# One branch for the whole of TensorE's program, in a macaron block (FFN, attention, FFN)

## The chip, the cores and the metric

The kernel runs on one core of a Trainium2 chip. The metric is the device time of one execution in microseconds (us); three executions of the kernel before gave 636.6, 638.17 and 639.28 us.

## The reference

`x` has 16 sequences of 256 tokens of 128 numbers, all fp32. Biases and weights are inputs; the FFN's weight matrices hold only -1, 0 and 1, each with a scale per output row.

```python
def ffn(x):                                   # _tlin(x, w, s) = einsum('bsi,oi->bso', x, w) * s
    h = silu(_tlin(x, w1_w, w1_s)) * _tlin(x, w2_w, w2_s)      # 128 -> 512
    h = gelu(_tlin(h, h1_w, h1_s), approximate=False)          # 512 -> 512
    h = gelu(_tlin(h, h2_w, h2_s), approximate=False)          # 512 -> 512
    return _tlin(h, w3_w, w3_s)                                # 512 -> 128
x = x + 0.5 * ffn(layernorm(x))
x = x + attention(layernorm(x))               # 16 heads of 8, softmax, projections Wq, Wk, Wv, Wo
x = x + 0.5 * ffn(layernorm(x))
```

## The kernel before

The program is written out by hand, engine by engine: each engine has one block of code, and semaphores join them. All 4096 tokens stay in SBUF (`X`). An FFN works on blocks of 512 tokens, two of them in one `body`; there are four bodies to an FFN, of which the middle two are the two trips of one loop (`Fori`). The attention between the two FFNs goes over 8 pairs of sequences; pairs 2 to 5 are two trips of another loop.

**Split products.** To keep fp32 accuracy each operand of an FFN product is a high part and a low part in a format that TensorE reads in one pass: `act_hi`, `act_lo` for activations, `WH`, `WL` for weights. `split_mm` (line 1014) multiplies `WH` by both parts of the activation. With `general=True` it multiplies `WL` by both as well, which doubles the matmuls. Weights of -1, 0 and 1 have a low part of zero, and then the second half can be left out.

**The flag.** Whether `WL` is all zero is found out while the kernel runs. VectorE takes the largest magnitude of `WL` per partition (`weight_lo_max`, `all_lo_max`), TensorE sums that over the partitions with one small matmul (line 1258), VectorE copies the sum to `flag` (line 730), and TensorE's sequencer loads it into the register `low_weights` (line 1263). The first block's layer 1 is issued ahead of that, always in the general form. Here the flag is zero.

**The branches.** TensorE's FFN code exists twice, as two copies in program order. `ffn_phase` (line 1246) ends in a compare on the register: `If_ne(low_weights, 0)` has the general copy (with `WL`) as its body and comes first in memory, `Else` has the short copy behind it. With a flag of zero the sequencer jumps over the general copy. `ffn_phase` is called once for each FFN, so this occurs twice: once behind the flag (here "branch 1"), once between attention and the second FFN ("branch 2"). Attention's code stands once, between the two. No other engine branches on the flag.

**What orders the work around the branches.** Ahead of branch 1 TensorE has nothing queued but the small sum, since `reg_load` waits for VectorE's copy. Behind it comes `hidden` (line 1048) of the first body: it waits for `h_full`, `h_lo` and `g_hi`, and ScalarE's Gelu (lines 534, 536) frees banks 4 and 5 for its third tile (line 1054). Ahead of branch 2 stand the last 16 `weigh` matmuls of attention (line 1129); behind it comes `layer1` (line 1027) of the second FFN, on `x_hi` and `x_lo` from lines 508 and 776. The sequencer can issue instructions ahead of the matmul array until a wait holds it. At the program's end SyncE stores the last rows of `X` (line 378) and all engines meet at a barrier.

Of the kernel before, what the change touches and what calls it, by code (L numbers as in the profile page):

```python
# [24 lines left out]
I32 = mybir.dt.int32  # L25
# [24 lines left out]
SKEW = 4  # L50
# [11 lines left out]
W_GROUPS = ((0, 1), (1, 2), (2, 3), (3, 5), (5, 7), (7, 9), (9, 11))  # L62
# [3 lines left out]
def macaron_kernel(nc, x, w_ffn, w_att, s12, sg, s3, bqk, bv, bo, eye, sel, low_rows, out):  # L66
# [3 lines left out]
    NBATCH = x.shape[0] // SEQ  # L70
    NPAIR = NBATCH // 2
# [6 lines left out]
    with ctx:  # L78
        def sb(name, shape, dt=F32, c=ctx):
            return c.enter_context(nc.sbuf_tensor(name, shape, dt))  # L80

        def sem(name):
            return ctx.enter_context(nc.semaphore(name))

        bank = [ctx.enter_context(nc.psum_tensor(f"bank{i}", [P, 512], F32)) for i in range(BANKS)]
# [14 lines left out]
        ONES = sb("ONES", [P, 1])  # L100
# [11 lines left out]
        lo_max = sb("lo_max", [P, len(W_GROUPS) + 1])  # L112
        flag = sb("flag", [1, 1])
# [14 lines left out]
        start = ExitStack()  # L128
# [29 lines left out]
        eye_in = sem("eye_in")  # L158
        att_in = sem("att_in")
        w_in = [sem(f"w_in{k}") for k in range(len(W_GROUPS))]  # L160
        ones_set = sem("ones_set")
# [3 lines left out]
        w_lo = sem("w_lo")  # L165
        w_lo_rest = sem("w_lo_rest")
        lo_reduced = sem("lo_reduced")
        flag_sum = sem("flag_sum")
        flag_set = sem("flag_set")
# [85 lines left out]
        def wait(eng, s, v):  # L255

            if not isinstance(v, int) or v > 0:
                eng.wait_ge(s, v)
# [750 lines left out]
        def _(pe):  # L1009
            T = nc.tensor  # L1010
            T.sem_inc(pv_mm, CREDIT)
            MM = T.matmul

            def split_mm(dst, w, xs, general):

                todo = [(wh, part) for (wh, _), (xh, xl) in zip(w, xs) for part in (xh, xl)]
                if general:
                    todo += [(wl, part) for (_, wl), (xh, xl) in zip(w, xs) for part in (xh, xl)]
                for k, (a, b) in enumerate(todo):  # L1020
                    ins = MM(dst, a, b, start=k == 0, stop=k == len(todo) - 1)  # L1021
                return ins

            def w_of(c, t):
                return WH[:, c, P * t:P * t + P], WL[:, c, P * t:P * t + P]

            def layer1(n0, nblk, general, between={}):

                for t in range(L1_TILES):
                    j, n = t // HT, n0 + t  # L1030
                    if t % HT == 0:
                        pe.wait_ge(xlo_done, nblk + j + 1)
                    xs = [(x_hi[:, j, :], x_lo[:, j, :])]

                    last = n - 3 if t >= 3 else n - 2
                    if t != 2:
                        wait(pe, silu_done, last + 1)
                    split_mm(bank[GATE_BANKS[t]][:, :], [w_of(C_W1, t % HT)], xs, general).then_inc(gate_mm, 1)
                    if t != 2:
                        wait(pe, h_full, last + 1)  # L1040
                    split_mm(bank[UP_BANKS[t]][:, :], [w_of(C_W2, t % HT)], xs, general).then_inc(up_mm, 1)
                    if t in between:
                        between[t]()
# [21 lines left out]
            def transpose_x(nx, j, to=None):  # L1065
                pe.wait_ge(xn_done, nx + 1)
                for t in range(TT):
                    ins = T.transpose(bank[to or 6 + j][:, P * t:P * t + P], xn[:, 4 * j + t, :], EYE[:, :])  # L1068
                ins.then_inc(xT_done, 1)
# [173 lines left out]
                    body(i)  # L1243
                body(NP - 1, more=False)

            def ffn_phase(f, low_weights):
                if f == 0:
                    pe.wait_ge(eye_in, 16)
                    transpose_x(0, 0)
                    transpose_x(1, 1)  # L1250

                    pe.wait_ge(w_lo, 2)
                    def sum_low_max():

                        pe.wait_ge(ones_set, 1)
                        pe.wait_ge(lo_reduced, len(W_GROUPS) + 1)
                        MM(bank[6][0:1, 0:1], ONES[:, 0:1], lo_max[:, len(W_GROUPS):len(W_GROUPS) + 1],
                           start=True, stop=True).then_inc(flag_sum, 1)
                    layer1(0, 0, True)  # L1260
                    sum_low_max()
                    pe.wait_ge(flag_set, 1)
                    pe.reg_load(low_weights, flag[0:1, 0:1].bitcast(I32))
                with pe.If_ne(low_weights, 0):
                    ffn_bodies(f, True)
                with pe.Else():
                    ffn_bodies(f, False)

            low_weights = T.alloc_register("low_weights")
            ffn_phase(0, low_weights)  # L1270

            def attend(b, pair, par, bb, prev=True, prev2=True, own=True, more=True, steps=UNITS,
                       ahead=None, v_pair=None):
# [75 lines left out]
            def att_body(i, par, ahead=True, more=True, first=False):  # L1349
                attend(2 * i, i, par, 0, prev=not first, prev2=not first, v_pair=i + 1 if more else None)  # L1350
                attend(2 * i + 1, i, par, 1, prev2=not first, more=more, ahead=i + 2 if ahead else None)

            att_body(0, 0, first=True)
            att_body(1, 1)
            with pe.Fori(1, NPAIR // 2 - 1) as n:
                att_body(2 * n, 0)
                att_body(2 * n + 1, 1)
            att_body(NPAIR - 2, 0, ahead=False)
            att_body(NPAIR - 1, 1, ahead=False, more=False)
            attend(NBATCH, NPAIR, 0, 0, own=False, more=False, steps=SKEW + 4)  # L1360
            ffn_phase(1, low_weights)

# [52 lines left out]
```

## Time and profile before

| | |
|---|---|
| runs of before | 636.6, 638.17, 639.28 us |
| profiled execution, its own time | 636.52 us |
| its span (first to last instruction) | 634.7 us |
| mean granted TensorE clock | 0.986 of full speed |
| PE busy | 597.0 us (94%) |
| ACT busy | 466.7 us (74%) |
| DVE busy | 436.8 us (69%) |
| POOL busy | 94.7 us (15%) |
| chain that ended last | PE 76%, DVE 8%, issue 7% |

PE is TensorE's matmul array and PEld its weight loads, DVE is VectorE, ACT ScalarE, POOL GpSimd, SP SyncE. A q behind a name (PEldq) is that engine's sequencer, whose branches, register loads and drains are recorded but are not counted as busy. "issue" as a releaser means that the engine waited for nothing that the profile shows. In the list of DMA queues, the kind `instruction` is the traffic that loads program code; q8 moved 31 packets of 16 KB.

### The profile page before, as it was taken

Reading aid. Unit: us, or ns where it says so; the run is one execution under the profiler, and the core shown is the slowest. Engines: PE = TensorE matmul, PEld = TensorE weight load, DVE = VectorE, ACT = ScalarE, POOL = GpSimd, SP = SyncE. Lnnn points to the kernel's source line nnn. Section 1 sums busy time; section 2 is a strip of 40 time slices with the busy share of each in tenths; the row PEclk is TensorE's granted clock in tenths of the full one; section 3 lists DMA queues with packets and bytes.
Section 4 is the critical chain, followed back from the end, with each engine's and each line's share of the span. In section 5 each row is a group of like instructions: output and inputs, shape, how many; then the busy total and the mean of one; then the engine's idle time right before and its main releaser. Section 6 shows DMA issues by size and latency. Waiting matters only on the chain.

```text
span 634.7 us, 12980 instructions
## 1 busy us (share of the span) xinstructions
PE 597.0 (94%) x4452; PEld 437.7 (69%) x4452; DVE 436.8 (69%) x1034; ACT 466.7 (74%) x793; POOL 94.7 (15%) x258
## 2 busy tenths in 40 slices
PE   1959999999999999999999999999899999999996
PEld 0738878878776675656656565666578878788785
DVE  4845485667835687979889898896385666855742
ACT  2746796787875568787878878787587877977964
POOL 2702001021010311222222222012001020020000
PEclk9979999999999979999999999999899999999999
DMA  8200000000034073434437062400000001000011
GB/s 287 69 2 2 0 1 1 2 0 0 1 133 133 24 242 124 144 136 133 165 104 263 36 229 106 162 2 2 3 2 0 1 1 35 0 6 27 1 33 35
DMA packets 36674, 41.97 MB, mean 66 GB/s; under 512 B 2448, under 2 KB 27280, under 8 KB 36624
## 3 DMA queue, kind: packets, MB, share of 16 engines
q1 hardware_dynamic: 36624, 41.31, 19.3%
q8 instruction: 31, 0.51, 0.3%
q14 instruction: 19, 0.16, 0.1%
HBM read 22.42 MB, written 18.87 MB: 65 GB/s over the span
## 4 chain that ended last, share of the span: by engine, by line
PE 76%; DVE 8%; issue 7%; POOL 3%; ACT 3%; DMA 2%; POOLq 0%; SPq 0%; DVEq 0%; ACTq 0%
PE bank L1021 48%; PE bank L1129 7%; PE bank L1104 6%; PE bank L1116 3%; PE bank L1118 2%; DVE neg_max L832 2%; PE bank L1161 2%; PE bank L1086 1%; PE bank L1090 1%; DVE act_lo L782 1%; PE bank L1068 1%; PE bank L1147 1%; PE bank L1139 1%; DMA QK<-qk_scratch 1%; DVE silu L791 1%
## 5 line engine op out<-in xcount | busy, mean ns | idle before, releaser
L1021 PE MATMUL bank<-act_hi,WH 128*128 128x512 f32 x576 | 233.1, 405 | 6.6 <-issue 5.3
L1021 PE MATMUL bank<-act_lo,WH 128*128 128x512 f32 x576 | 228.3, 396 | 0.0
L832 DVE TENSOR_REDUCE neg_max<-bank 128x2 f32<-128x512 f32 x256 | 166.2, 680 | 31.8 <-PE bank L1104 30.2
L802 DVE TENSOR_TENSOR act_lo<-full,act_hi 128x512 fp32r<-128x512 f32 x128 | 87.8, 688 | 123.2 <-ACT act_hi L536 123.0
L647 ACT ACTIVATE probs<-bank 128x512 f32<-128x512 f32 x256 | 139.3, 597 | 34.1 <-PE bank L1118 32.3
L534 ACT ACTIVATE full<-bank,SG 128x512 f32<-128x512 f32 x128 | 88.1, 688 | 70.0 <-PE bank L1021 69.6
L1021 PEld LDWEIGHTS bank<-act_hi,WH 128*128 128x128 f32 x576 | 108.7, 189 | 36.8 <-issue 5.9
L1021 PEld LDWEIGHTS bank<-act_lo,WH 128*128 128x128 f32 x576 | 108.8, 189 | 25.1 <-issue 0.5
L1116 PE MATMUL bank<-QK 32*128 32x256 f32 x512 | 93.1, 331 | 0.9 <-DVE m_parts L838 0.5
L536 ACT ACTIVATE act_hi<-bank,SG 128x512 fp32r<-128x512 f32 x128 | 87.4, 683 | 0.0
L1118 PE MATMUL bank<-m_parts,SEL 32*128 32x256 f32 x512 | 79.3, 277 | 0.0
L1104 PE MATMUL bank<-QK 32*128 32x256 f32 x512 | 74.3, 331 | 1.8 <-DVE neg_max L832 1.2
L1104 PEld LDWEIGHTS bank<-QK 32*128 32x128 f32 x512 | 46.1, 185 | 40.4 <-issue 21.1
L1129 PE MATMUL bank<-probs,V 128*32 128x256 f32 x1024 | 69.9, 391 | 0.0
L1116 PEld LDWEIGHTS bank<-QK 32*128 32x128 f32 x512 | 61.4, 185 | 3.6 <-ACT probs L647 2.1
L1118 PEld LDWEIGHTS bank<-m_parts,SEL 32*128 32x128 f32 x512 | 61.9, 187 | 0.0
L791 DVE SCALAR_TENSOR_TENSOR silu<-bank,S,silu 128x512 f32<-128x512 f32 x64 | 47.1, 743 | 16.4 <-ACT silu L521 15.9
L1021 PE MATMUL bank<-x_hi,WH 128*128 128x512 f32 x128 | 51.7, 404 | 2.1 <-issue 1.6
L1021 PE MATMUL bank<-x_lo,WH 128*128 128x512 f32 x128 | 51.1, 399 | 0.0
L521 ACT ACTIVATE silu<-bank,S 128x512 f32<-128x512 f32 x64 | 43.1, 683 | 9.5 <-PE bank L1021 9.5
L399 POOL TENSOR_TENSOR newton<-rstd 128x8 f32<-128x8 f32 (+1 forms) x45 | 11.9, 265 | 241.0 <-DVE rstd L762 238.7
L782 DVE TENSOR_TENSOR act_lo<-silu,act_hi 128x512 fp32r<-128x512 f32 x64 | 45.5, 710 | 0.2
(91 smaller groups left out, 593.2 us busy)
## 6 DMA issues: line engine op xcount, KB each, us to landing
qk_scratch<-qk SPq DMA_DIRECT2D x64, 256.0 KB, 2.6
QK<-qk_scratch SPq DMA_DIRECT2D x16, 1024.0 KB, 7.1
X<-x SPq DMA_DIRECT2D x4, 512.0 KB, 7.2
raw_rest<-w_ffn SPq DMA_DIRECT2D x4, 512.0 KB, 6.0
out<-X SPq DMA_DIRECT2D x4, 512.0 KB, 3.2
raw<-w_ffn SPq DMA_DIRECT2D x3, 256.0 KB, 4.5
WA<-w_att SPq DMA_DIRECT2D x1, 256.0 KB, 5.4
xT<-sel SPq DMA_DIRECT2D x1, 256.0 KB, 5.4
```

The source lines that it names most:

```text
L534: A.activation(full[:, t, :], bank[4 + t % 2][:, :], ACT.Gelu, scale=SG[:, layer, t:t + 1])
L536: A.activation(act_hi[1 + layer][:, j, t, :], bank[4 + t % 2][:, :], ACT.Gelu, scale=SG[:, layer, t:t + 1]).then_inc(g_hi, 1)
L647: A.activation(probs[:, v % 8, :], bank[B_BANKS[bb][v]][:, :], ACT.Exp, scale=SCALE)\
L782: D.tensor_tensor(act_lo[0][:, t // HT, t % HT, :], silu[:, t % SLOTS, :], act_hi[0][:, t // HT, t % HT, :].bitcast(F32), op=ALU.subtract)\
L791: D.scalar_tensor_tensor(out=silu[:, t % SLOTS, :], in0=bank[UP_BANKS[t]][:, :], scalar=S12[:, 1, t % HT:t % HT + 1], in1=silu[:, t % SLOT ...
L802: D.tensor_tensor(act_lo[1 + layer][:, j, t, :], full[:, t, :], act_hi[1 + layer][:, j, t, :].bitcast(F32), op=ALU.subtract)\
L832: D.tensor_reduce(neg_max[:, bb, qt, n0:n0 + 2], bank[(banks or A_BANKS[bb])[u]][:, :].rearrange("p (h k) -> p h k", h=2), axis=AX.X, op=A ...
L1021: ins = MM(dst, a, b, start=k == 0, stop=k == len(todo) - 1)
L1104: ins = MM(bank[banks[u]][:, SEQ * i:SEQ * i + SEQ], q_of(2 * par + bb)[rows, 2 * jj + i, P * qt:P * qt + P], k_of(2 * par + bb)[rows, 2 * ...
L1116: MM(dst, k_of(2 * par + bb)[rows, 2 * jj + i, P * kt:P * kt + P], q_of(2 * par + bb)[rows, 2 * jj + i, :], start=True, stop=False)
L1118: ins = MM(dst, SEL[rows, 2 * jj + i, :], m_parts[rows, bb, :], start=False, stop=True)
L1129: ins = MM(bank[4][32 * h:32 * h + 32, SEQ * (g // 3):SEQ * (g // 3) + SEQ], V[par][:, VROW * (2 * bb + kt) + col:VROW * (2 * bb + kt) + c ...
```

## The change

`ffn_phase` goes. A new function `all_layers(general)` holds the first FFN's bodies, the whole of attention and the second FFN's bodies, and it is written out twice. There is one compare, behind the flag, and its sense is turned: `If_eq(low_weights, 0)` has the short copy as its body, first in memory, and `Else` has the general copy. Nothing else in the kernel is touched; `attend` and `att_body` stay as they are and are only called from another place.

```diff
-            def ffn_phase(f, low_weights):
-                if f == 0:
-                    pe.wait_ge(eye_in, 16)
...
-                    layer1(0, 0, True)
-                    sum_low_max()
-                    pe.wait_ge(flag_set, 1)
-                    pe.reg_load(low_weights, flag[0:1, 0:1].bitcast(I32))
-                with pe.If_ne(low_weights, 0):
-                    ffn_bodies(f, True)
-                with pe.Else():
-                    ffn_bodies(f, False)
...
-            ffn_phase(0, low_weights)
...
-            att_body(0, 0, first=True)
...
-            attend(NBATCH, NPAIR, 0, 0, own=False, more=False, steps=SKEW + 4)
-            ffn_phase(1, low_weights)
+            def all_layers(general):
+                ffn_bodies(0, general)
+                att_body(0, 0, first=True)
+                att_body(1, 1)
+                with pe.Fori(1, NPAIR // 2 - 1) as n:
+                    att_body(2 * n, 0)
+                    att_body(2 * n + 1, 1)
+                att_body(NPAIR - 2, 0, ahead=False)
+                att_body(NPAIR - 1, 1, ahead=False, more=False)
+                attend(NBATCH, NPAIR, 0, 0, own=False, more=False, steps=SKEW + 4)
+                ffn_bodies(1, general)
...
+            layer1(0, 0, True)
+            sum_low_max()
+            pe.wait_ge(flag_set, 1)
+            pe.reg_load(low_weights, flag[0:1, 0:1].bitcast(I32))
+            with pe.If_eq(low_weights, 0):
+                all_layers(False)
+            with pe.Else():
+                all_layers(True)
```

**Branch 1, on TensorE, before.** `bank4` takes the first tile of the first hidden layer; the rows between are the same pair for the other three blocks of the sum.

```order
L1258 MATMUL bank6<-lo_max,ONES 1x1
L1263 TENSOR_LOAD flag
L1264 COMPARE_AND_BRANCH
L1021 MATMUL bank4<-act0_hi,WH 128x512
L1021 MATMUL bank4<-act0_lo,WH 128x512
...
L1021 MATMUL bank4<-act0_hi,WL 128x512
L1021 MATMUL bank4<-act0_lo,WL 128x512
```

**Branch 1, on TensorE, of the change.**

```order
L1251 MATMUL bank6<-lo_max,ONES 1x1
L1356 TENSOR_LOAD flag
L1357 COMPARE_AND_BRANCH
L1021 MATMUL bank4<-act0_hi,WH 128x512
L1021 MATMUL bank4<-act0_lo,WH 128x512
...
L1021 MATMUL bank5<-act0_hi,WH 128x512
L1021 MATMUL bank5<-act0_lo,WH 128x512
```

Before, the general copy (with `WL`) follows the compare, and the copy that runs here stands 1,062 rows of the list further on. In the change the copy that runs here follows the compare at once.

**Branch 2, on TensorE, before.** The end of attention and layer 1 of the second FFN; `probs,V1` are the `weigh` matmuls of the last sequence but one step.

```order
L1154 MATMUL bank6<-EYE,o_nat 128x128 x2
L1161 MATMUL bank6<-WA,onT 128x128 x2
L1129 MATMUL bank4<-probs,V1 32x256 x8
L1264 COMPARE_AND_BRANCH
L1021 MATMUL bank0<-x_hi,WH 128x512
L1021 MATMUL bank0<-x_lo,WH 128x512
L1021 MATMUL bank0<-x_hi,WL 128x512
```

**The same place in the change.**

```order
L1154 MATMUL bank6<-EYE,o_nat 128x128 x2
L1161 MATMUL bank6<-WA,onT 128x128 x2
L1129 MATMUL bank4<-probs,V1 32x256 x8
L1021 MATMUL bank0<-x_hi,WH 128x512
L1021 MATMUL bank0<-x_lo,WH 128x512
L1021 MATMUL bank2<-x_hi,WH 128x512
```

The compare has gone, and the short form of layer 1 follows attention directly.

**The end of the copy that runs here, in the change.** The last transposes of the output, and what follows them in memory.

```order
L1074 MATMUL bank6<-EYE,yT 128x128 x4
L1074 MATMUL bank7<-EYE,yT 128x128 x4
L1357 UNCONDITIONAL_BRANCH
L1021 MATMUL bank4<-act0_hi,WH 128x512
```

The short copy now ends in a branch over the whole general copy (3,349 rows of the list) to the program's end. Before, the short copy of the second FFN was the last thing in TensorE's program.

## Rows read from the trace of the kernel before

**Rows 1.** The page's first part: busy time, share of the span, instructions.
```profile
PE 597.0 (94%) x4452; PEld 437.7 (69%) x4452; DVE 436.8 (69%) x1034; ACT 466.7 (74%) x793; POOL 94.7 (15%) x258
```

**Rows 2.** What PE waited for: releaser, us in total, times, longest us.
```profile
PE bank L1068 <- DVE xn L770: 13.4, 1, 13.4
PE bank L1021 <- issue: 6.9, 2, 5.3
PE bank L1139 <- POOL neg_max L450: 2.8, 6, 0.8
```

**Rows 3.** Timeline at branch 1: start, us, engine, line [idle before <-releaser].
```profile
33.18 0.74 DVE L791 SCALAR_TENSOR_TENSOR silu<-bank,S,silu 128x512 f32<-128x512 f32 x1
34.73 0.19 PE L1258 MATMUL bank<-lo_max,ONES 128*1 128x1 f32 x2 [1.72 <-DVE lo_max L725]
35.77 0.14 DVE L730 COPY flag<-bank 1x1 f32<-1x1 f32 x1
40.25 0.76 PE L1021 MATMUL bank<-act_hi,WH 128*128 128x512 f32 x1 [5.32 <-issue]
...
43.80 0.49 PE L1021 MATMUL bank<-act_hi,WH 128*128 128x512 f32 x1
44.07 1.28 ACT L534 ACT_TABLE_LOAD   x1 [8.16 <-PE bank L1021]
45.36 0.69 ACT L534 ACTIVATE full<-bank,SG 128x512 f32<-128x512 f32 x1
45.95 0.68 ACT L536 ACTIVATE act_hi<-bank,SG 128x512 fp32r<-128x512 f32 x1
46.68 0.51 PE L1021 MATMUL bank<-act_hi,WH 128*128 128x512 f32 x1 [0.76 <-ACT act_hi L536]
```

**Rows 4.** Both compares on the flag, and the flag's load: ns min/median/max, first and last start.
```profile
L1264 PEldq COMPARE_BRANCH  x2: 3300/3440/3579, 36.5 to 451.3; - x2
L1263 PEldq TENSOR_LOAD <-flag x1: 492/492/492, 35.9 to 35.9; - x1
```

**Rows 5.** The loops' compares on PE's sequencer, FFN and attention, same columns.
```profile
L1242 PEldq COMPARE_BRANCH  x4: 76/156/243, 125.8 to 591.1; - x4
L1355 PEldq COMPARE_BRANCH  x2: 83/159/235, 335.4 to 392.8; - x2
```

**Rows 6.** DMA queues in 36 to 42 us: queue, kind, packets, MB.
```profile
q8 instruction: 2, 0.03, 2.2%
```

**Rows 7.** DMA queues in 334 to 395 us, all that moved anything.
```profile
q1 hardware_dynamic: 7031, 9.44, 44.2%
```

**Rows 8.** Timeline at branch 2.
```profile
449.34 0.69 DVE L776 TENSOR_TENSOR x_lo<-bank,x_hi 128x512 fp32r<-128x512 f32 x1 [0.29 <-ACT x_hi L508]
450.09 1.28 ACT L521 ACT_TABLE_LOAD   x1
451.27 1.94 PE L1129 MATMUL bank<-probs,V 128*32 128x256 f32 x16
454.76 0.47 PE L1021 MATMUL bank<-x_hi,WH 128*128 128x512 f32 x1 [1.56 <-issue]
455.50 0.69 ACT L521 ACTIVATE silu<-bank,S 128x512 f32<-128x512 f32 x1 [4.13 <-PE bank L1021]
```

**Rows 9.** PE's busy time and clock by stretch: us, busy (x), PEclk, DMA share, GB/s.
```profile
37.20:40.20 3.00, 0.00 (x0) 0.50 0.02 5
40.25:43.90 3.65, 3.65 (x9) 0.50 0.02 4
44.00:46.00 2.00, 1.92 (x8) 1.00 0.00 0
450.20:453.50 3.30, 3.01 (x20) 0.50 0.02 7
60.00:120.00 60.00, 59.98 (x271) 1.00 0.00 1
```

**Rows 10.** The end: timeline, the last store's landing, and the drains at the barrier.
```profile
629.52 0.66 PE L1074 MATMUL bank<-EYE,yT 128*128 128x128 f32 x4 [0.34 <-ACT yT L543]
631.11 0.38 SPq L378 DMA_DIRECT2D out<-X  x1
L78 PEldq DRAIN  x1: 700/700/700, 629.5 to 629.5; - x1
L78 SPq DRAIN  x1: 7/7/7, 634.5 to 634.5; - x1
```

More of the change, by code:

```diff
@@ L1244, in ffn_bodies, with sum_low_max @@
                 body(NP - 1, more=False)
-            def ffn_phase(f, low_weights):
-                if f == 0:
-                    pe.wait_ge(eye_in, 16)
[L1249 to L1259, printed above, removed]
-                    layer1(0, 0, True)
-                    sum_low_max()
-                    pe.wait_ge(flag_set, 1)
-                    pe.reg_load(low_weights, flag[0:1, 0:1].bitcast(I32))
-                with pe.If_ne(low_weights, 0):
-                    ffn_bodies(f, True)
-                with pe.Else():
-                    ffn_bodies(f, False)
-            low_weights = T.alloc_register("low_weights")
-            ffn_phase(0, low_weights)
+            def sum_low_max():
+                pe.wait_ge(ones_set, 1)
+                pe.wait_ge(lo_reduced, len(W_GROUPS) + 1)
+                MM(bank[6][0:1, 0:1], ONES[:, 0:1], lo_max[:, len(W_GROUPS):len(W_GROUPS) + 1],
+                   start=True, stop=True).then_inc(flag_sum, 1)
             def attend(b, pair, par, bb, prev=True, prev2=True, own=True, more=True, steps=UNITS,
@@ L1351, in att_body @@
                 attend(2 * i + 1, i, par, 1, prev2=not first, more=more, ahead=i + 2 if ahead else None)
-            att_body(0, 0, first=True)
[L1354 to L1359, printed above, removed]
-            attend(NBATCH, NPAIR, 0, 0, own=False, more=False, steps=SKEW + 4)
-            ffn_phase(1, low_weights)
+            def all_layers(general):
[9 more added lines that the diff above has]
+                ffn_bodies(1, general)
+            low_weights = T.alloc_register("low_weights")
+            pe.wait_ge(eye_in, 16)
+            transpose_x(0, 0)
+            transpose_x(1, 1)
+            pe.wait_ge(w_lo, 2)
+            layer1(0, 0, True)
[6 more added lines that the diff above has]
+                all_layers(True)
 def kernel(**inputs):
```

## The prediction, made before the changed kernel was run

> **What bounds the kernel now.** I read the busy shares first. PE is busy 597.0 of 634.7 us, 94% of the span, with 4,452 matmuls [rows 1]. TensorE is the bound, and 37.7 us of idleness are all there is to win without touching its matmuls. Then I read what PE waited for [rows 2]. The largest entry, 13.4 us, is the start (loads and the first layer norm), which the change doesn't touch. The next is "issue", 6.9 us in only two pieces, 5.32 and 1.56 us. "issue" means that no semaphore explains it, so the reason has to be sought in the instruction stream. The timeline puts one at 40.25 us, right behind the flag [rows 3], the other at 454.76 us, between attention and the second FFN [rows 8]. These are the places of the two compares on the flag. The sequencer's own records then give the cause its size: the two compares take 3579 ns (at 36.5 us) and 3300 ns (at 451.3 us) [rows 4]. The reader should set beside them the loops' compares on the same engine. In each group one execution goes back to the loop's head and the next leaves the loop: maxima of 243 and 235 ns, minima of 76 and 83 ns [rows 5]. So a compare that falls through costs about 80 ns, a short jump back about 240 ns, and only the long jump over the general copy costs 3.3 to 3.6 us.
>
> What is in these 3.3 to 3.6 us? In 36 to 42 us the queue that loads program code moves two packets of 16 KB [rows 6]. The whole second trip of the attention loop, 334 to 395 us, has no such packet at all [rows 7], although its body is hundreds of matmuls long. I read that as: code that lies behind the sequencer is still there, code that lies far ahead has to be fetched when the jump is taken, and the sequencer stands still meanwhile.
>
> **Branch 1, step by step.** The flag's copy starts at 35.77 us, the register load at 35.9 takes 492 ns, the compare starts at 36.50 and ends 3.58 us later, at 40.08 [rows 3, 4]. The first matmul behind it starts at 40.25, 0.17 us on. In the change the copy that runs follows the compare. It takes 0.08 us as the loops' exits do, so the first matmul starts at 36.50 + 0.08 + 0.17 = 36.75 us: 3.50 us earlier. Nothing else is late at that time. `hidden` needs the sixth product of layer 1, done at 33.18 + 0.74 = 33.92 us [rows 3]; its low parts for the first block are older.
>
> What follows is a chain from PE's first tile: 8 matmuls, then ScalarE's table load (1.28 us, which starts only when the tile is there), two Gelu passes, and PE's third tile at 46.68 us, which waits 0.76 us for them [rows 3]. From the first matmul to that is 46.68 - 40.25 = 6.43 us. It moves as a whole if the tile takes as long as before. Its 8 matmuls ran at half clock: the granted clock was 0.50 from 37.2 to 43.9 us after PE had stood idle, and 1.00 from 44.0 [rows 9]. At 0.50 they took 43.80 - 40.25 = 3.55 us; at full clock, by the 60 us stretch with 271 matmuls in 59.98 us (0.221 us each) [rows 9], they take 1.8 us. With a shorter pause the clock may fall as before, or not fall. Two ends: the second tile also runs slow and its 8 matmuls last past the Gelu, some 3.55 + 3.55 - 6.43 = 0.7 us lost; or the first tile runs fast, 3.55 - 1.8 = 1.75 us won. I take 0: PE is idle here for nearly 4 us in the change too, and the row that I have shows a fall. Branch 1 gives 3.5 us, between 2.8 and 5.2.
>
> **Branch 2.** The compare starts at 451.29 and ends at 454.59, but PE still has 16 queued matmuls until 451.27 + 1.94 = 453.21 us [rows 4, 8]. That covers 1.9 us of the jump, and 1.56 us are left bare. Without a compare layer 1 starts at 453.2. Its input `x_lo` was ready at 449.34 + 0.69 = 450.03, and ScalarE's table load, which would be next late, ended at 451.37 [rows 8]. ScalarE and VectorE wait 4.13 us here for PE [rows 8], so they move with it. The clock stood at 0.50 until 453.5 [rows 9], so a first matmul may run slow at a cost of 0.2 us. Branch 2 gives 1.5 us, between 1.2 and 1.6.
>
> **Does the gain last?** Between the two PE is saturated (59.98 of 60 us in mid-FFN [rows 9]), and every other engine is released by PE's results. The loads of the start were done before 36 us. An earlier PE thus moves everything behind it by the same amount.
>
> **The end.** The short copy now ends in a long jump. PE's sequencer is through at 629.5 us and drains in 0.70 us [rows 10]. A jump of 3.3 to 3.6 us brings it to 633.1 at most, its drain no later than 633.8. The barrier waits for the last store anyway: issued at 631.11, SyncE's drain at 634.5 [rows 10]. 0.7 us of cover are left, all of it shifted alike by the gains above. I cost the jump at 0; bare, it would cost at most what it takes beyond 4.3 us. Attention's second copy is never executed and costs nothing but memory.
>
> **Sum.** 3.5 + 1.5 = 5.0 us from this execution's span of 634.7 gives 629.7, and from its own time of 636.52 gives 631.5. This execution lies 1.65 us below the median of the runs, 638.17. From the median the same gain gives 633.2 us, 0.8% faster.
>
> **A figure that speaks against it.** The Trainium skill ("Advanced Engine Details and Errata", Control Flow Timing) gives a compare-and-branch about 108 ns. By that figure two compares are worth 0.2 us, and the change nothing. The loops' rows of 76 to 243 ns are near it, the two rows of 3300 and 3579 ns are not, so the trace disagrees where the jump is long. The skill's "Runtime: NRT & Kernel Launch", Instruction fetch mechanics, says that a taken branch forces a fetch when its target is outside a window of two pages. The trace agrees on the fetch but not on so small a window: an attention trip of 57 us came back to its head in 235 ns without a packet.
>
> **Rivals.**
> 1. *The compare's time is not the jump* but the price of a compare right after work that was waited for, and stays where it is at branch 1. For: branch 1 stands behind a register load. Against: branch 2 has no load ahead of it and costs 3.30 us all the same [rows 4]. Or the code right behind branch 1 is not loaded yet; against that, no code packet is asked for until 37 us, and none of the many later steps from one packet's code to the next shows as "issue" [rows 2]. Either way only branch 2 is won: 638.2 - 1.5 = 636.7 us, "no change". Chance 0.08.
> 2. *A cheap compare.* The two pauses are something else that stays, and the time is 638.2 us. It is the result that the 108 ns of the page would give. The pairing of rows 4 with both "issue" gaps speaks against it. Chance 0.03.
> 3. *Loops that lose their code* (the slower side). The loops now lie elsewhere. If their heads had been dropped when they branch back, each of the three back edges (125.8, 335.4, 548.0 us) would cost 3.3 to 3.6 us instead of 0.24, of which PE's queue covers up to 1.9 us: 1.4 to 3.3 us bare, 4.2 to 9.9 us in three. Against a gain of 5.0 this gives -0.8 to +4.9 us, in the middle 640 us. It makes the kernel slower by over 3.2 us when more than 2.7 us a back edge are bare. It is what the skill's window of two pages would do to any body longer than that. For it: nothing in the trace. Against: the bodies keep their length, and the longest came back in 235 ns [rows 5, 7]. Chance 0.03.
> 4. *The end comes bare*: the last jump's fetch runs beside the last store and takes 2 us longer than its cover. The gain is then 3.0 us, 635.2 us. Chance 0.06.
>
> **How the numbers follow.** My forecast, both gaps gone, has 0.80. About 0.5% (3.2 us) is what a measurement of this kernel can tell from no change. The forecast's own range of gains is 4.0 to 6.8 us by the bounds above; nearly all of it lies beyond 3.2 us, but the three runs of before spread by 2.7 us, so I keep 0.03 of it for "same". Faster: 0.77 + 0.03, half of rival 4, = 0.80. Same: 0.03 + 0.08 (rival 1) + 0.03 (rival 2) + 0.03 (the other half of rival 4) = 0.17. Slower: 0.03 (rival 3). The range runs from 638.2 - 6.8 - 0.4 for the runs' spread = 631.0 to 636.8, which takes in rivals 1 and 4.
>
> **What would show it right or wrong.** In the changed kernel's records the one compare on the flag should last about 0.1 us; the gap behind the small sum should be about 1.8 us in place of 5.32, the gap behind the last `weigh` matmuls gone, and "issue" no longer among PE's largest waits. An unconditional branch of 3 to 4 us should stand at the end, with PE's drain before SyncE's. The loops' maxima should stay near 240 ns. A compare that is still over 3 us long, loop compares of over 1 us, or PE's drain as the last at the barrier would each refute a step. The forecast fails as a whole if the span is above 632 us.

## The result, and the profile after

| | runs | median us | ratio to before, 95% interval |
|---|---|---|---|
| before | 5 | 638.17 | |
| the change | 5 | 630.43 | 0.9881 [0.9852, 0.9909] |
| before, measured again | 19 | 637.16 | |
| the change, measured again | 6 | 630.32 | 0.9908 [0.9885, 0.9931] |

The change makes the kernel 0.9 to 1.2% faster in the two measurements, 6.8 to 7.7 us between medians. I had forecast 633.2 us, 5.0 us faster, with a low end of 631.0: the direction was right, the size too small, and the time lies below my range. The first profiled execution of the change took 645.56 us, and the ratio leaves it out; what happened in it is told below. The rows here are from the profiled execution of the second measurement, with a span of 627.9 us against 634.7.

What PE waited for there (us in total, times, longest us), to be read against [rows 2]:

```profile
PE bank L1068 <- DVE xn L770: 13.3, 1, 13.3
PE bank L1139 <- POOL neg_max L450: 2.9, 6, 0.8
PE bank L1251 <- DVE lo_max L725: 1.9, 1, 1.9
PE bank L1021 <- DVE silu L791: 1.8, 1, 1.8
```

"issue" has left the list. In its place at branch 1 stands a gap of 1.8 us, put down to a VectorE product. In truth it is the way of the sum through the flag's copy on VectorE, the register load and the compare. The sequencer's compares, to be read against [rows 4, 5], and the drains at the end against [rows 10]:

```profile
L1357 PEldq COMPARE_BRANCH  x2: 93/1892/3692, 36.5 to 622.7; - x2
L1242 PEldq COMPARE_BRANCH  x4: 76/153/233, 122.1 to 584.3; - x4
L1339 PEldq COMPARE_BRANCH  x2: 83/152/220, 331.4 to 388.8; - x2
L78 PEldq DRAIN  x1: 67/67/67, 626.5 to 626.5; - x1
L78 SPq DRAIN  x1: 7/7/7, 627.7 to 627.7; - x1
```

The compare on the flag takes 93 ns at 36.5 us. The record of 3692 ns at 622.7 us is the branch over the general copy at the end. It is through before PE's drain at 626.5, 1.2 us ahead of SyncE's, so it is hidden.

The two places, on PE's timeline and ScalarE's (start, us, engine, line [idle before <-releaser]), against [rows 3, 8]:

```profile
34.69 0.19 PE L1251 MATMUL bank<-lo_max,ONES 128*1 128x1 f32 x2 [1.95 <-DVE lo_max L725]
36.72 0.76 PE L1021 MATMUL bank<-act_hi,WH 128*128 128x512 f32 x1 [1.84 <-DVE silu L791]
...
40.33 1.28 ACT L534 ACT_TABLE_LOAD   x1 [4.46 <-PE bank L1021]
...
42.94 0.50 PE L1021 MATMUL bank<-act_hi,WH 128*128 128x512 f32 x1 [0.82 <-ACT act_hi L536]
...
446.93 1.07 PE L1129 MATMUL bank<-probs,V 128*32 128x256 f32 x16
447.93 0.50 PE L1021 MATMUL bank<-x_hi,WH 128*128 128x512 f32 x1
```

The first hidden tile starts at 36.72 us (forecast 36.75) in place of 40.25, and the third at 42.94 in place of 46.68: 3.74 us won. At branch 2 layer 1 starts 1.00 us behind the start of the last `weigh` matmuls, in place of 454.76 - 451.27 = 3.49 us. The `weigh` group itself takes 1.07 us, not 1.94: its clock was whole here.

The two traces also tell where the gain comes in. The change leads by 3.74 us at the third tile, by 451.27 - 446.93 = 4.34 us at the last `weigh` group, and by 454.76 - 447.93 = 6.83 us at layer 1 of the second FFN. The spans differ by the same 6.8 us, so the whole gain is there once branch 2 has been passed, and 2.49 us of it come at branch 2 itself. The 0.6 us between the two branches fall partly where before ran at half clock already (450.2 to 453.5 us [rows 9]) and the change did not.

### The profile page after: what moved, and what is told of

Same layout as the page of the kernel before. It is cut to its first block, busy times and chain, and to the rows that moved or that the text cites. A ratio compares the mean times of both kernels' runs of the same rounds, so it can differ in the third digit from the quotient of the medians.

```text
span 643.8 us, 12980 instructions
## 1 busy us (share of the span) xinstructions
PE 604.8 (94%) x4452; PEld 443.5 (69%) x4452; DVE 437.8 (68%) x1034; ACT 466.4 (72%) x793; POOL 94.7 (15%) x258
## 4 chain that ended last, share of the span: by engine, by line
PE 73%; DVE 7%; issue 7%; DMA 4%; POOL 3%; ACT 3%; SPq 1%; POOLq 0%; DVEq 0%; ACTq 0%
PE bank L1021 47%; PE bank L1129 6%; PE bank L1104 6%; PE bank L1116 3%; PE bank L1118 2%; DMA QK<-qk_scratch 2%; DVE neg_max L832 2%; PE bank L1161 1%; PE bank L1086 1%; PE bank L1068 1%; SPq L340 1%; PE bank L1090 1%; DVE silu L791 1%; DVE act_lo L782 1%; PE bank L1139 1%
## 5 line engine op out<-in xcount | busy, mean ns | idle before, releaser
L1116 PE MATMUL bank<-QK 32*128 32x256 f32 x512 | 97.0, 341 | 0.9 <-DVE m_parts L838 0.5
L1104 PE MATMUL bank<-QK 32*128 32x256 f32 x512 | 77.1, 341 | 8.9 <-issue 6.7
L1118 PE MATMUL bank<-m_parts,SEL 32*128 32x256 f32 x512 | 82.4, 285 | 0.0
L1104 PEld LDWEIGHTS bank<-QK 32*128 32x128 f32 x512 | 48.4, 193 | 48.9 <-issue 27.8
L1116 PEld LDWEIGHTS bank<-QK 32*128 32x128 f32 x512 | 64.2, 193 | 3.7 <-ACT probs L647 2.1
L1118 PEld LDWEIGHTS bank<-m_parts,SEL 32*128 32x128 f32 x512 | 64.9, 196 | 0.0
```

The costliest lines, as they stand in the source:

```text
L1104: ins = MM(bank[banks[u]][:, SEQ * i:SEQ * i + SEQ], q_of(2 * par + bb)[rows, 2 * jj + i, P * qt:P * qt + P], k_of(2 * par + bb)[rows, 2 * ...
L1116: MM(dst, k_of(2 * par + bb)[rows, 2 * jj + i, P * kt:P * kt + P], q_of(2 * par + bb)[rows, 2 * jj + i, :], start=True, stop=False)
L1118: ins = MM(dst, SEL[rows, 2 * jj + i, :], m_parts[rows, bb, :], start=False, stop=True)
```

## The experiments

Each kernel is given by its edit; all medians are device times of one execution.

**The change once more.** No edit.

> The changed kernel once more, for its usual time and a second trace. In its first profiled execution (span 643.8 us) the compare at the end of the attention loop's first trip took 5113 ns instead of 235 ns, with code packets all through the second trip, and TensorE's clock then stood at half for 20 us. Theory L (layout): the loop now lies so that its code and the block fetched ahead of it don't fit at once, in every execution; then this trace shows the compare at 3 to 5 us again, and the median of 630.4 us contains that loss. Theory C (chance): it was an accident of that one execution; then this trace shows about 235 ns, no code packet in the second trip, and a span of 627 to 630 us. Theory K (clock): what the change gained beyond 5.0 us is less time at half clock after shorter pauses; then the mean granted clock is above 0.986 here, and span differences follow it.

Median 630.32 us (629.69 to 633.64), before 637.16 beside it. The attention loop's compare took 220 ns (row above), so "in every execution" of theory L is refuted. Theory K holds in part: this trace has a mean clock of 0.991 against 0.986. Grouping the executions by their mean clock gives a rough split. At 0.989, before has spans of 634.4 us (mean of 16) and the change, padded or not, 628.55 us (mean of 4): 5.9 us are gone at equal mean clock. The other 1 us goes with a higher mean clock, 0.9889 against 0.9853 over 16 and 42 executions. But the mean counts idle time too. Before stood at half clock for some 3 us in which PE did nothing (37.2 to 40.2 us [rows 9]); by an estimate, half of 3 us over a span of 634.7 us, that alone lowers its mean by 0.0024 and costs nothing. So how much of the last 1 us is the clock's is not shown.

**One branch, general copy first.**

```diff
-            with pe.If_eq(low_weights, 0):
-                all_layers(False)
-            with pe.Else():
-                all_layers(True)
+            with pe.If_ne(low_weights, 0):
+                all_layers(True)
+            with pe.Else():
+                all_layers(False)
```

> One branch only, but with the general copy first and the old sense (If_ne): branch 1 keeps its long jump, branch 2 is gone, the end needs no jump. By the prediction's steps 1.5 us under before, 636.7 us, with a compare of 3.3 to 3.6 us at 36.5 us. If branch 1 is worth more than its 3.5 us through the clock, this kernel stands 5 us or more above the changed one; if the extra gain comes from having one branch at all, it is within 3 us of the changed one.

634.50 us (633.23 to 636.06), ratio 0.9953 [0.9937, 0.997]. Branch 2 alone is worth 637.16 - 634.50 = 2.7 us, not 1.5; branch 1 is the remaining 4.2 us, between the two cases that I had set (5 us or more, and within 3 us). The 2.7 us can't be put down to the mean clock: this kernel idles at branch 1 as before does, and at a mean clock of 0.989 its two executions have spans of 631.6 us, 2.8 us under before's 634.4. The compare at branch 1 is as long as ever:

```profile
L1357 PEldq COMPARE_BRANCH  x1: 3686/3686/3686, 36.4 to 36.4; - x1
```

PE's timeline at the place where branch 2 was:

```profile
451.10 1.16 PE L1161 MATMUL bank<-WA,onT 128*128 128x128 f32 x4 [0.62 <-ACT onT L661]
452.19 1.94 PE L1129 MATMUL bank<-probs,V 128*32 128x256 f32 x16
454.05 0.74 PE L1021 MATMUL bank<-x_hi,WH 128*128 128x512 f32 x1
```

In this execution the clock was at half here although there is no jump, so the fall of the clock at attention's end is not the jump's doing. It comes in some executions and not in others. With it layer 1 starts 1.86 us behind the `weigh` group's start, without it 1.00 us.

**Before, moved by 70 instructions.**

```diff
                     pe.wait_ge(eye_in, 16)
+                    for _ in range(140):
+                        pe.wait_ge(eye_in, 16)
```

 Theory L: its compare at the loop's end rises from 235 ns to 3 to 5 us, code packets appear in the second trip, and the time rises by 2 to 5 us to 640 to 643 us, more where the clock falls. Theory C: no difference, 638 us, and 235 ns.

639.29 us (636.53 to 649.27), ratio 1.0028 [1.0006, 1.005]: slower than before by little, between the values of the two theories. The loop's compare took 231 ns in the profiled execution (640.00 us), so the miss did not come there. Three of the 12 executions took 642.21, 642.85 and 649.27 us; they have no trace, so whether the miss came in them is open. By the count of instructions the loop's end lies 4 short of where I wanted it, at the edge and not beyond it; the kernel tests theory L badly. Its trace is worth more at branch 2. PE's timeline, and then its clock by stretch (us, busy, PEclk):

```profile
453.19 1.07 PE L1129 MATMUL bank<-probs,V 128*32 128x256 f32 x16
456.92 0.77 PE L1021 MATMUL bank<-x_hi,WH 128*128 128x512 f32 x1 [2.66 <-issue]
```

```profile
456.80:459.90 3.10, 2.98 (x7) 0.50 0.03 5
460.30:462.00 1.70, 1.70 (x11) 1.00 0.00 0
```

Here the `weigh` group runs at full clock and is over after 1.07 us. So the jump's bare part is 2.66 us in place of 1.56 [rows 2, 8], and the clock is at half behind it, when layer 1 starts. From the group's start to layer 1 it is 3.73 us (before: 3.49). This is what branch 2 costs: the sequencer's 3.3 to 3.5 us set that interval in both traces, with the `weigh` group at half clock in one and at full clock in the other.

**The change, moved by 40 instructions.**

```diff
             pe.wait_ge(eye_in, 16)
+            for _ in range(80):
+                pe.wait_ge(eye_in, 16)
             transpose_x(0, 0)
```

> The changed kernel with 80 waits on a semaphore that is already up, at TensorE's start, where it is idle until 13.3 us: they cost nothing and move all later code by 40 instructions, so that the attention loop crosses one fetch boundary fewer (6 as before, not 7). Theory L: the compare at the attention loop's end falls from 3 to 5 us to about 0.24 us, the second trip has no code packets, and the time falls by 2 to 5 us under the changed kernel, to 626 to 628 us. Theory C: no difference, 630 us within noise.

630.56 us (628.39 to 631.41): no difference from the change, as it has to be if the change's usual executions don't miss either. Loop compare 222 ns.

**The change, moved by 16 instructions.** The same edit with 32 waits.

> The changed kernel moved by only 16 instructions (32 waits at TensorE's idle start). In the changed kernel a fetch boundary falls within a few instructions of the attention loop's closing compare, by counting instructions and by when the code packets came; here it falls some 16 ahead of it in every execution, while the loop's head stays in the same block as in the changed kernel. Theory L (the loop's code plus the block fetched ahead exceed what TensorE keeps): each execution now misses at the back edge: a compare of 3 to 5 us in the first trip's end, 7 more code packets in the second trip, and a median of 633 to 645 us. Theory C (the miss in the change's first profiled execution was unrelated to layout): 235 ns, 630.5 us.

641.28 us (639.21 to 648.6) in 12 executions, ratio 1.0067 [1.0036, 1.0098]: slower than before, and some 11 us above the change. Even the fastest is 5.6 us above the slowest of the change's ten other executions (633.64). The profiled execution, the only one with a trace: first the loop's compare, then what PE waited for and the first matmul behind the jump, then the code packets from 334 to 402 us and from 337.9 to 341.7 us, then the clock by stretch:

```profile
L1339 PEldq COMPARE_BRANCH  x2: 83/2371/4659, 333.2 to 402.6; - x2
```

```profile
PE bank L1104 <- issue: 7.6, 1, 7.6
341.74 0.57 PE L1104 MATMUL bank<-QK 32*128 32x256 f32 x1 [7.64 <-issue]
```

```profile
q8 instruction: 8, 0.13, 0.8%
q8 instruction: 1, 0.02, 1.5%
```

```profile
336.40:353.00 16.60, 11.26 (x92) 0.50 0.55 182
354.00:370.00 16.00, 15.93 (x206) 1.00 0.01 2
```

The jump back to the loop's head takes 4659 ns, eight packets of code come in the second trip where before had none [rows 7], and PE stands bare for 7.6 us. The jump explains only the first half of that: it ends at 333.16 + 4.66 = 337.8 us, and the next matmul comes 3.9 us later. One more packet of code comes in that second half. That the block behind the head's was missing as well is my reading of it; no run shows it apart. The clock stays at half for some 17 us, to 353 us at least. In the first profiled execution of the change the jump back takes longer still, and PE stands bare twice, for 4.48 and 2.17 us:

```profile
L1339 PEldq COMPARE_BRANCH  x2: 83/2598/5113, 333.2 to 404.2; - x2
338.62 0.57 PE L1104 MATMUL bank<-QK 32*128 32x256 f32 x1 [4.48 <-issue]
342.14 0.37 PE L1104 MATMUL bank<-QK 32*128 32x256 f32 x1 [2.17 <-issue]
336.50:356.80 20.30, 16.01 (x116) 0.50 0.48 156
```

So theory L holds with one correction: in the change a fetch boundary falls on the loop's last instructions, and by their times (645.56 us against 628.70 to 633.64) the miss came in 1 of its 11 executions; 16 instructions further on the median is 11 us higher; 40 further on, by the count, the head has moved into the next block too, and the usual time is back. No experiment shows what decides it at the edge from one execution to the next.

**Before with only branch 2 turned.**

```diff
+                if f == 0:
+                    with pe.If_ne(low_weights, 0):
+                        ffn_bodies(f, True)
+                    with pe.Else():
+                        ffn_bodies(f, False)
+                else:
+                    with pe.If_eq(low_weights, 0):
+                        ffn_bodies(f, False)
+                    with pe.Else():
+                        ffn_bodies(f, True)
```

> The kernel before with only branch 2 turned to If_eq, so that it is still there but falls through. Theory J (only the long jump costs): branch 2 lasts about 0.08 us and the kernel equals the one with one branch and the general copy first, which measured 634.5 us. Theory N (a compare of any kind stops TensorE's queue): it stays at before's 637.2 us.

634.80 us (633.69 to 638.2), before 638.03 on the same chip at the same time, ratio 0.9961 [0.9939, 0.9982]: 3.2 us, as with no branch 2 at all (0.9953). A compare that falls through costs PE nothing here. It takes 79 ns at 451.8 us, and layer 1 starts 1.00 us behind the `weigh` group's start, as in the change. The 3474 ns are its jump at the end, hidden.

```profile
L1270 PEldq COMPARE_BRANCH  x2: 79/1776/3474, 451.8 to 627.6; - x2
451.79 1.07 PE L1129 MATMUL bank<-probs,V 128*32 128x256 f32 x16
452.79 0.50 PE L1021 MATMUL bank<-x_hi,WH 128*128 128x512 f32 x1
```

**Both branches kept, both turned.** `If_eq` with the short copy first in `ffn_phase`, for both FFNs.

> Both branches kept and both turned to If_eq. Both compares fall through; in exchange the first FFN's short copy ends in a long jump to attention, behind the transposes of its last output. Theory J: the two compares take under 0.1 us, the new jump 3.3 to 3.8 us on the sequencer, of which TensorE's queue covers little there; so one jump price comes back and the time is 633 to 635 us, 3 to 4 us above the changed kernel. If the sense of the branch alone carried the gain, it would be 630.5 us.

630.89 us (628.75 to 632.0), ratio 0.9884 [0.9851, 0.9916]: the change's own time. My forecast of a jump price at the end of the first FFN was wrong. The jump is there (four records at this line, the longest 3839 ns), but on PE's timeline it leaves no "issue":

```profile
L1264 PEldq COMPARE_BRANCH  x4: 75/1864/3839, 36.6 to 625.0; - x4
215.15 1.09 PE L1074 MATMUL bank<-EYE,yT 128*128 128x128 f32 x8
217.44 0.51 PE L1104 MATMUL bank<-QK 32*128 32x256 f32 x4 [1.19 <-DVE neg_max L832]
218.02 0.41 PE L1139 MATMUL bank<-EYE,neg_max 128*128 128x128 f32 x2
```

The same place in the change:

```profile
216.73 0.51 PE L1104 MATMUL bank<-QK 32*128 32x256 f32 x4 [0.44 <-DVE neg_max L832]
218.06 0.41 PE L1139 MATMUL bank<-EYE,neg_max 128*128 128x128 f32 x2 [0.83 <-POOL neg_max L450]
```

The jump starts at 213.25 us, while PE has work until 215.15 + 1.09 = 216.24; 1.2 us are left bare. The change waits there for other engines anyway, 0.44 and 0.83 us, and the matmul behind starts at 218.06 us with no jump and at 218.02 with it. One branch in place of two is therefore not what gained: which copy stands first is.

**A version that beats both.** The first seven matmuls of the first hidden tile are the same in both copies. They go ahead of the small sum and the flag, and the copies begin with the eighth (on top of the move by 40).

```diff
+            def hoisted():
+                pe.wait_ge(silu_done, 6)
+                pe.wait_ge(h_lo, HT)
+                pe.wait_ge(g_hi, 1)
+                w = [w_of(C_H1 + k, 0) for k in range(HT)]
+                todo = [(wh, part) for (wh, _), (xh, xl) in zip(w, inputs_of(0, 0)) for part in (xh, xl)]
+                for k, (a, b) in enumerate(todo[:HOISTED]):
+                    MM(bank[4][:, :], a, b, start=k == 0, stop=False)
...
             layer1(0, 0, True)
+            hoisted()
             sum_low_max()
```

> A version meant to beat both: the changed kernel, moved by 40 instructions as in the padded version, with the first 7 matmuls of the first hidden tile (they are the same in both copies) issued ahead of the small sum and the flag, into the 1.7 us in which TensorE waits for the largest low part. The tile is then complete 0.2 us behind the branch instead of 3.6, so ScalarE's table load and Gelu start earlier. By the second trace of the changed kernel: its first tile ends at 40.3, here at about 37.2, so third tile and all behind it come 2.5 to 3.1 us earlier, and 627.5 to 628.5 us. If a clock that falls later takes the gain back (TensorE still idles 1.8 us for the flag), 629.5 us.

627.81 us (627.1 to 628.92), ratio 0.9849 [0.9817, 0.988]: 2.5 to 2.8 us under the medians of the change and of its move by 40 instructions, which were taken on another chip, where before had 637.16 and not 638.03 us. That is within what I expected. PE and ScalarE:

```profile
34.22 0.40 PE L1034 MATMUL bank<-act_hi,WH 128*128 128x512 f32 x1
34.58 0.19 PE L1264 MATMUL bank<-lo_max,ONES 128*1 128x1 f32 x2
36.60 0.47 PE L1024 MATMUL bank<-act_lo,WH 128*128 128x512 f32 x1 [1.83 <-DVE silu L791]
37.14 1.28 ACT L534 ACT_TABLE_LOAD   x1 [1.39 <-PE bank L1024]
40.01 0.63 PE L1024 MATMUL bank<-act_hi,WH 128*128 128x512 f32 x1
```

The seven matmuls fill the wait for the largest low part and delay the sum by nothing; the table load starts at 37.14 in place of 40.33 us, and the third tile at 40.01 in place of 42.94.

## Why the prediction was right in kind and too small

- **What the time is: right.** Both "issue" gaps belonged to the long jump. The two compares fell from 3.3 and 3.6 us to 93 ns and nothing, and in the three kernels that vary the layout (general copy first, only branch 2 turned, both turned) the compares on the flag took 3556 and 3686 ns with the general copy first and 75 to 101 ns with the short one first.
- **Branch 1: right.** 3.5 us forecast, 3.53 us at the first matmul, 3.74 at the third tile in the traces. Between medians it is 4.2 us (634.50 - 630.32), or 3.9 (634.80 - 630.89, with branch 2 turned in both); that the rest comes through the clock is argued, not shown.
- **Branch 2: the term that was mis-sized, and the step that failed.** I took the bare gap of the one trace, 1.56 us, as what would be won ("1.5 us, between 1.2 and 1.6"). But the cover that I subtracted, 1.9 us of `weigh` matmuls, was that long only because the clock stood at half, and I even saw that in [rows 9]. The jump's start and end are set by the sequencer. Where the clock is whole, the same matmuls cover 1.0 us and the jump leaves 2.5 (3.49 - 1.00) to 2.7 us bare; where it is at half, 1.6 us (3.49 - 1.86). The medians give 2.7 and 3.2 us, 1.2 to 1.7 us more than the term; the whole gain was 1.8 to 2.7 us larger than forecast. With 2.5 in place of 1.5 the sum is 6.0 us, near the 5.9 us at equal mean clock, though that rough measure splits the 5.9 into 2.8 for branch 2 and 3.1 for branch 1.
- **The clock behind a jump: left out.** I weighed it at branch 1 and took 0, and at branch 2 I counted only a loss. In the traces with a far jump at 36 us it stood at half there for 6.8 to 10.2 us, in those without for 3.4 to 6.8; and in the padded kernel before it was at half from 456.8 us, behind the jump at 453. It also differed from trace to trace where the code is the same: at attention's end it fell without any jump in two traces. So that shorter pauses save clock fits the higher mean (0.9889 against 0.9853) and the last 1 us, but no run shows how much of it they carry.
- **The end: right.** 3.7 us of jump, 1.2 us of cover left.
- **Rival 3 had chance 0.03 and happened**, at one of its three places and in one execution of eleven. Its dismissal, "the bodies keep their length", was the mistake: a body of 6.2 blocks touches 7 or 8 of them, depending on where it starts. I had [rows 7] to say that it fitted once, and didn't ask for its position. Its price was also too low: I gave a back edge 1.4 to 3.3 us, and the one that missed left PE bare for 6.7 us (4.48 + 2.17) and 7.6 us, with 17 to 20 us at half clock behind it, 11 us between medians.
- **Rivals 1, 2 and 4** are refuted by the compare of 93 ns, by the medians, and by the drains.

## What to carry to other kernels

Read the sequencer's own records where "issue" stands in front of a matmul: a compare that falls through costs 0.1 us, a far jump 3.3 to 3.8 us, so the copy that usually runs should come first (no run here has a jump forward into code that is already held), and its exit jump belongs where the engine waits anyway or at the end. When an edit removes a stall, don't subtract the cover as it was clocked beside the stall: take the interval that the sequencer set, less the same work at full clock. And where a loop's code fills most of what the engine keeps, its position counts: a shift by 16 instructions cost this kernel 11 us.

## What the runs showed of the hardware

- A compare on PE's sequencer took 67 to 101 ns falling through and 212 to 245 ns going back to a loop's head whose code was still held. A far jump took 3300 to 3846 ns, and the two that missed at a loop's head took 4659 and 5113 ns.
- PE came back to a loop head 57 us old without a packet. By a count of the built program the body has 1,579 instructions, and a packet of 16 KB follows about every 256 of them. The first trip asked for 6 packets in the traces of before and of the change that hit, and the miss came where a seventh followed, 0.3 and 0.5 us behind the start of the compare. The change moved by 40 has a seventh too, 0.8 us behind its compare, and hits; this fits only because, by the count, its head lies one block further on. An estimate from all this is that PE keeps 8 blocks, the one being fetched ahead among them. The Trainium skill ("Runtime: NRT & Kernel Launch", Instruction fetch mechanics) speaks of a window of two pages; these traces refute that for TensorE, though not the fetch on a taken branch.
- After the bare 7.6 us at the missed back edge the clock stood at half for some 17 us (PE was busy for 11.26 of 16.60 us of them), and from 354 us on it was whole.
